# First layer of a four-layer decoder: the end of the gated delta rule moves from a block of its own into the rounds of the loop before it

## The reference, cut to what matters

```
z = (hidden_states @ W_z).reshape(b_, t_, HV, DV)
...
o = oT.transpose(1, 0, 2, 3)
var = jnp.mean(o * o, axis=-1, keepdims=True)
o = o * jax.lax.rsqrt(var + EPS) * norm_w * jax.nn.silu(z)
return o.reshape(b_, t_, V_DIM) @ W_out
```

## Time and profile before

| what | us |
|---|---|
| time, median of 3 runs (lowest to highest) | 4789.43 (4788.31 to 4794.76) |
| profiled execution, its own time | 4789.89 |
| its span, first to last instruction | 4788.2 |
| TensorE, VectorE, ScalarE, GpSimd busy | 4042.8, 2461.2, 1544.0, 820.0 |
| from the end of the loop's last write of `v` to L195's start, first pass | 350.28 to 383.22 |

### The profile page before, as it was taken

The page is one execution under the profiler, slowest core; times in us unless marked ns, Lnnn a source line. Parts: engine busy times, 40 slices in busy tenths (PEclk is TensorE's granted clock), DMA queues, the critical chain, the costliest instruction groups (busy, mean ns, idle before and its releaser), DMA issues. The chain is left out here.

```text
span 4788.2 us, 96589 instructions
## 1 busy us (share of the span) xinstructions
PE 4042.8 (84%) x38364; PEld 2472.2 (52%) x38364; DVE 2461.2 (51%) x6030; ACT 1544.0 (32%) x3476; POOL 820.0 (17%) x1436
## 2 busy tenths in 40 slices
PE   6997787898799778789879987878987998787888
PEld 3883343465388334346548733434654873343465
DVE  5664444454566453445456645335545664533554
ACT  3442222341344222234234422223413542222341
POOL 1430000130143000013014300001201430001120
PEclk7999999999799999999979999999997999999999
DMA  2000000000000000000000010000000001000000
GB/s 79 3 3 16 41 18 17 22 35 25 25 3 3 22 36 18 17 22 35 25 25 3 3 56 1 18 18 22 35 25 25 3 3 56 1 18 18 22 35 27
DMA packets 11005, 105.56 MB, mean 22 GB/s; under 512 B 1148, under 2 KB 5552, under 8 KB 6192
## 3 DMA queue, kind: packets, MB, share of 16 engines
q1 hardware_dynamic: 10544, 99.21, 5.4%
HBM read 98.16 MB, written 1.05 MB: 21 GB/s over the span
## 5 line engine op out<-in xcount | busy, mean ns | idle before, releaser
L88 PE MATMUL psum<-ident_bf 128*128 128x512 bf16 x1880 | 522.1, 416 | 206.6 <-DVE l_attn_peak L770 66.9
L88 PEld LDWEIGHTS psum<-ident_bf 128*128 128x128 bf16 x1880 | 184.6, 106 | 471.4 <-issue 161.8
L2926 DVE TENSOR_TENSOR l_attn_xx<-l_attn_xx,psum 128x256 f32<-128x256 f32 x512 | 205.8, 418 | 205.5 <-PE psum L2633 193.0
L2747 ACT ACTIVATE l_attn_ax<-psum 128x128 f32<-128x128 f32 (+1 forms) x768 | 184.9, 279 | 357.1 <-PE psum L2614 242.7
L399 DVE TENSOR_TENSOR l_ffn_hidden<-l_ffn_silu,psum 128x512 f32<-128x512 f32 (+2 forms) x184 | 126.2, 686 | 323.2 <-ACT l_ffn_silu L340 323.1
L94 PEld LDWEIGHTS psum<-streamed_weights,l_ffn_hidden 128*128 128x128 f32 (+2 forms) x1728 | 225.9, 192 | 115.6 <-issue 98.8
L340 ACT ACTIVATE l_ffn_silu<-psum 128x512 f32<-128x512 f32 (+2 forms) x216 | 128.9, 597 | 473.6 <-PE psum L310 473.3
L2629 PE MATMUL psum<-l_attn_ax,l_attn_xx 64*64 64x64 f32 x5120 | 265.0, 222 | 0.0
L2633 PE MATMUL psum<-l_attn_xx,l_attn_ax 64*64 64x64 f32 x5120 | 258.2, 219 | 0.0
L770 DVE TENSOR_REDUCE l_attn_peak<-psum 128x4 f32<-128x2048 f32 (+3 forms) x128 | 185.7, 1487 | 121.2 <-PE psum L688 120.2
L2824 POOL TENSOR_TENSOR l_attn_part<-l_attn_ab,streamed_weights 128x128 f32<-128x128 f32 x640 | 242.6, 415 | 27.4 <-PE psum L2614 27.4
(11 more groups left out here) (514 smaller groups left out, 8146.2 us busy)
## 6 DMA issues: line engine op xcount, KB each, us to landing
streamed_weights<-pack_l_ffn SPq DMA_DIRECT2D x4, 5412.0 KB, 15.7
streamed_weights<-pack_l_ffn SPq DMA_DIRECT2D x4, 3972.0 KB, 12.6
streamed_weights<-pack_l_attn SPq DMA_DIRECT2D x5, 2848.5 KB, 9.5
streamed_weights<-pack_l_xattn SPq DMA_DIRECT2D x4, 2496.0 KB, 8.6
streamed_weights<-pack_l_ffn SPq DMA_DIRECT2D x4, 2192.0 KB, 8.3
streamed_weights<-pack_l_xattn SPq DMA_DIRECT2D x4, 2048.0 KB, 8.5
streamed_weights<-pack_l_ffn SPq DMA_DIRECT2D x4, 1923.0 KB, 8.0
streamed_weights<-pack_l_attn SPq DMA_DIRECT2D x4, 1107.5 KB, 5.0
```

Source lines behind the costliest of these rows:

```text
L88: pe.matmul(self.bank(bank), self.ident_bf[:, :], self.ident_bf[:, :].unsqueeze(1).to_broadcast([P, NT, P]), start=True, stop=True)
L2747: act.activation(ax[b, p, :, :], m.psum[b, p, 0:P].rearrange("p (i t) -> p i t", i=2), ACT.Copy).then_inc(ax_ready, 1)
L2926: dve.tensor_tensor(both, both, m.psum[:, p, P:384], ALU.subtract).then_inc(x_less, 1)
```

## The change

The second block is gone. Its work is written into the order of rounds 2 to 8, and what is left runs after the loop within the same block. The `warm` matmuls are gone too.

- GpSimd: `squares(n - 2)`, 512 columns, at level 1 of rounds 2 to 7, between the `part` of levels 1 and 2; `squares(6)` and `squares(7)` after the loop's rounds.
- VectorE: `reduce(n - 2)` at level 2 of rounds 2 to 8, behind `prep(n + 1, FIRST)` and ahead of the `output` and the subtraction of level 3. In round 7, `roots` of tiles 0 to 2 (48 columns) follow at level 2, `scale(0)` at level 3, `gated(0)` and `scale(1)` at level 4, `scale(2)` at level 5; in round 8, `gated(1)` at level 2 and `gated(2)` at level 4. Behind the loop: `reduce(7)`, `roots` of tile 3, and `scale` and `gated` of it in two halves.
- TensorE: `gate` (one half tile of `z`) twice at level 1 and once each at levels 3 and 5 of round 7, twice each at levels 2 and 5 of round 8; `turn_y` twice each at levels 1 and 4 of round 8. Behind the loop `turn_y(2)`, `project` of tiles 0 to 2, `turn_y(3)`, `project(3)`. Gates and turned outputs share banks 4 and 5 by turns, in the order of the list `LATE`.
- ScalarE: Silu of the gates in round 7 at levels 2, 3, 4 and 6, and in round 8 behind `corrected`; the copies of the turned outputs in round 8 at levels 1 and 4, between `ks` and `corrected`.
- `z` and the turned outputs use buffers of the loop that are free by then.

```diff
+                def gate(t, half):
+                    n = LATE.index(("z", t, half))
+                    if n >= 2:
+                        pe.wait_ge(late_read, n - 1)
+                    pe.matmul(m.bank(4 + n % 2), m.xnT[:, tok(t)], w["z"][:, 512 * half:512 * half + 512], start=True,
+                              stop=True).then_inc(late_psum, 1)
+
+                def turn_y(t, half):
+                    n = LATE.index(("y", t, half))
+                    pe.wait_ge(y_ready, t + 1 + (half if t == NT - 1 else 0))
+                    pe.wait_ge(late_read, n - 1)
+                    for c in range(4):
+                        ins = pe.transpose(m.psum[:, 4 + n % 2, tok(c)], v[:, t, tok(4 * half + c)], m.ident)
+                    ins.then_inc(late_psum, 1)
+
+                def project(t):
+                    pe.wait_ge(late_read, LATE.index(("y", t, 1)) + 1)
+                    for c in reversed(range(8)):
+                        pe.matmul(m.psum[:, OUT, tok(t)], yT[t][:, c, :], w["out"][:, c, :],
+                                  start=t == 0 and c == 7, stop=c == 0, skip_group_check=True)
...
+                def squares(n):
+                    t, g_ = divmod(n, 2)
+                    o = v[:, t, 8 * W * g_:8 * W * g_ + 8 * W]
+                    pool.wait_ge(o_ready, unit(n, 3) + 1)
+                    if n >= 1:
+                        pool.wait_ge(reduced, n)
+                    pool.tensor_tensor(square[:, :], o, o, ALU.mult).then_inc(square_ready, 1)
...
+                def reduce(n):
+                    dve.wait_ge(square_ready, n + 1)
+                    dve.tensor_reduce(var[:, 8 * n:8 * n + 8], square[:, :].rearrange("p (h v) -> p h v", v=W), AX,
+                                      ALU.add).then_inc(reduced, 1)
...
+                        if n >= 2 and l == 2:
+                            reduce(n - 2)
+                        if n == STEPS - 1 and l == 2:
+                            roots(0, NT - 1)
+                        elif n == STEPS - 1 and l == 3:
+                            scale(0)
+                        elif n == STEPS - 1 and l == 4:
+                            gated(0)
+                            scale(1)
+                        elif n == STEPS - 1 and l == 5:
+                            scale(2)
+                        elif n == STEPS and l == 2:
+                            gated(1)
+                        elif n == STEPS and l == 4:
+                            gated(2)
+                reduce(STEPS - 1)
+                roots(NT - 1, NT)
+                for half in range(2):
+                    scale(NT - 1, slice(8 * half, 8 * half + 8))
+                    gated(NT - 1, slice(8 * half, 8 * half + 8))
```

More of the change, by code:

```diff
@@ L2684, in _ @@
                             past(n, add, SECOND)
+                        if n == STEPS - 1 and l == 1:
+                            gate(0, 0)
+                            gate(0, 1)
+                        elif n == STEPS - 1 and l == 3:
+                            gate(1, 0)
+                        elif n == STEPS - 1 and l == 5:
+                            gate(1, 1)
+                        elif n == STEPS and l == 1:
+                            turn_y(0, 0)
+                            turn_y(0, 1)
+                        elif n == STEPS and l == 2:
+                            gate(2, 0)
+                            gate(2, 1)
+                        elif n == STEPS and l == 4:
+                            turn_y(1, 0)
+                            turn_y(1, 1)
+                        elif n == STEPS and l == 5:
+                            gate(3, 0)
+                            gate(3, 1)
+                turn_y(2, 0)
+                turn_y(2, 1)
+                pe.wait_ge(o_ready, UNITS)
+                for t in range(NT - 1):
+                    project(t)
+                for half in range(2):
+                    turn_y(NT - 1, half)
+                project(NT - 1)
             @block.scalar
@@ L2788, in _ @@
                             ks(n - 1, SECOND)
+                        if n == STEPS - 1 and l == 2:
+                            gate(0, 0)
+                        elif n == STEPS - 1 and l == 3:
+                            gate(0, 1)
+                        elif n == STEPS - 1 and l == 4:
+                            gate(1, 0)
+                        elif n == STEPS - 1 and l == 6:
+                            gate(1, 1)
+                        elif n == STEPS and l == 1:
+                            copy_y(0, 0)
+                            copy_y(0, 1)
+                        elif n == STEPS and l == 2:
+                            gate(2, 0)
+                            gate(2, 1)
+                        elif n == STEPS and l == 4:
+                            copy_y(1, 0)
+                            copy_y(1, 1)
+                        elif n == STEPS and l == 5:
+                            gate(3, 0)
+                            gate(3, 1)
+                for t in (NT - 2, NT - 1):
+                    for half in range(2):
+                        copy_y(t, half)
             @block.gpsimd
@@ L2825, in _ @@
                                                over_block(w["levels"][:, l, :]), ALU.mult).then_inc(part_ready, 1)
+                        if l == 1 and n >= 2:
+                            squares(n - 2)
                         if l == 2 and n + 1 < STEPS:
@@ L2833, in _ @@
                             mask(n + 1, SECOND)
+                squares(STEPS - 2)
+                squares(STEPS - 1)
             @block.vector
@@ L2967, in _ @@
                             add(n - 1, SECOND)
-        mid.close()
[L2970 to L2982, removed]
@@ L3044, in stage_l0_attn @@
+                reduce(STEPS - 1)
+                roots(NT - 1, NT)
+                for half in range(2):
+                    scale(NT - 1, slice(8 * half, 8 * half + 8))
+                    gated(NT - 1, slice(8 * half, 8 * half + 8))
+        mid.close()
     return None
```

112 lines of the change are left out of this document (54 added, 58 removed).

## The result

| what | us |
|---|---|
| changed kernel, median of 4 runs (lowest to highest) | 4738.0 (4730.73 to 4747.60) |
| kernel before on the same chip, 4 runs | 4788.87 (4782.75 to 4794.76) |
| ratio, 95% interval | 0.9899 (0.9877 to 0.9921) |
| profiled execution of the changed kernel, own time and span | 4747.60 and 4745.9 |
| changed stage, first level-1 half of round 0 to the next L195, four passes | 248.74, 248.77, 248.55, 248.80 |

The changed kernel is 50.9 us faster, 4738.0 where 4734 was forecast. Its profiled execution is the slowest of its four. The stage starts at 121.72 there and at 119.04 in before, so its first pass begins 2.68 us later than that of before.

The account below looks back on a forecast made before the run. TensorE bounds the loop; behind it 32.94 us are nearly all one chain. With 2.05 us for the rounds, L195 at 369.4 instead of 383.22 saves 13.8 a pass, 55.3 in four, from 4789.89: 4734.6, as median 4734.1; range 4724 to 4756.

Parts of the forecast that it names:

- Squares on GpSimd, 0: Rounds 2 to 7: squares behind level 1's parts on GpSimd cost 0, or 1 us a round if the cover were gone.
- Nothing is late: Rounds 2 to 7: the squares on GpSimd delay no later work, a cost of 0.
- The cover I named: GpSimd idles 7.3 us behind level 2's parts, which are ready at 285.2 and read by the half at 292.4.
- The sum, 0.27 in each of five rounds: Rounds 2 to 6: VectorE's sum takes 0.62, GpSimd's parts cover 0.35, about 0.27 stays; 1.35 us, bounds 0 and 3.1.
- Contention, +0.14 a round: Rounds 2 to 6: squares push GpSimd's parts under both L2868 on VectorE, 0.14 more each round, 0.7 us in all.
- the 2.05 us that I charged to rounds 2 to 6: Rounds 2 to 6 a pass: 1.35 us for the sums plus 0.7 us for contention.
- Rounds 7 and 8: Added gates, roots and products make `r` of FIRST 4.36 later; last `v` at 354.1 instead of 350.28, at full clock.
- The clock: TensorE's clock stays 1.00 from 340 to 366, where before it falls at about 340.9 in round 8.
- Rival A: TensorE's clock falls in round 8: 7.4 us a pass, 29.4 in four, total 4764; chance 0.30.
- Rival B: VectorE's work isn't hidden up to `r` of round 7: 8.7 us more a pass, 35 in four, total 4769; chance 0.12.
- C: Roots make TensorE wait in round 7, clock falls and stays low until the projection: 13 us slower, 4802; chance 0.06.
- Behind the loop: From last `v` at 354.1: tile 3 ready 361.2, three projections done 362.3, last projection ends 366.05, next stage 367.35.

Follow-up runs that it names:

- Sum at level 1: Changed kernel with the sum of rounds 2 to 7 at level 1 instead of level 2 on VectorE: 4710.2 us, ratio 0.9848 to the kernel before.
- sum twice: Changed kernel with each level 2 sum of rounds 2 to 7 done twice on VectorE: 4741.1 us, ratio 0.9898 to the kernel before.
- squares late: Changed kernel with the squares of rounds 2 to 7 behind the sums of level 2 on GpSimd: 4716.8 us, ratio 0.9852 to the kernel before.
- thin round 8: Changed kernel with round 8's turned outputs, gates, their copies and gated(2) moved behind its work: 4749.0 us, ratio 0.992 to the kernel before.
- products behind: Changed kernel with roots and products of tiles 0 to 2, turned outputs and copies behind the loop: 4781.5 us, ratio 0.9985 to the kernel before.

## Why the prediction was right, point by point

**Squares on GpSimd, 0.** Right in size. But "Nothing is late" left out that the squares wait for the outputs of SECOND (2.67 us) and hold the next parts back by that. The cover I named was there: the parts of level 2 are ready at 292.05, and the half that reads them starts at 295.37.

**The sum, 0.27 in each of five rounds.** Measured 0.27 in round 6 by the idle time ahead of level 4's half. Sum at level 1 gives back 0.25 to 0.26 in rounds 2 and 4 to 6 but 0.58 in round 3, and sum twice shows that no cover is left for a second one in the same four rounds. So the term is right for four of the five rounds; round 3 went its own way in both runs.

**Contention, +0.14 a round: wrong in sign.** The step "the squares push the parts of level 2 under both L2868 of a round" failed. The waiting squares push them beyond both: the first fell from 0.42 to 0.29, and the round gained 0.12 to 0.16. This gain begins at the end of round 1, which is 0.16 shorter. The mechanism itself, a VectorE instruction with two operands in SBUF that runs long while GpSimd works, is borne out by squares late (0.41 again). How long depends on where it begins: at level 3, L2868 began 0.08 us into a single GpSimd part of 0.42 in round 6 and took 0.48; the sum pushes its successor L2986 to 0.31 us into one of 0.41, and it takes 0.28. The roots in round 7 (0.42 and 0.33 beside GpSimd against 0.19) ran long too, with one operand. The Trainium skill (GPSIMD Engine Reference, Specifications) says that GpSimd shares its SBUF interfaces with VectorE and names two cases of contention: VectorE instructions with two SBUF inputs, and those in a 2-port mode. By that rule L2986 agrees (0.41 beside GpSimd, 0.29 alone); the first two instructions of the roots have a single input, so they fall under it only if they ran in such a mode, which no run here shows. Of the 2.05 us that I charged to rounds 2 to 6, the start of round 7 shows 0.44 (197.32 us behind the first half, 196.88 before; 0.23 to 0.62 in the other passes). By the rounds that is five sums at 0.27 less six gains of 0.15.

**Rounds 7 and 8.** From the start of round 7 to the end of the last `v` 38.09 us passed, 38.18 were forecast. `r` of FIRST starts 28.03 us into round 7, where the schedule (343.75 on before's 315.92) had 27.83. The 3.5 us of the roots came out at 3.44. From the stage's start `r` of FIRST is 5.0 us later than before, where 6.4 was forecast.

**The clock.** 1.00 from 340 to 366 as forecast. Rival A was a real mechanism and not a wrong fear: thin round 8 and products behind bring it back. Its price of 7.4 us was not measured by itself. Rival B charged 15.1 us up to `r` of FIRST and is out by the 5.0 measured; products behind puts roots and four products at 0.73 of them. C is out by the clock.

**Behind the loop.** 13.33 us from the end of the last `v` to L195, forecast 13.25. By its parts: tile 3 ready 7.3 us behind the last `v` (7.1), the third projection done 8.2 behind it (8.2), the last projection 2.05 (1.85). The forecast's terms (362.3, 1.0, 0.77, 1.85) add up to 365.92 and not to the 366.05 written, so that 0.13 of the agreement is a slip.

**The sum.** The stage gained 15.4 us a pass, 13.8 were forecast: 1.6 more, which is the 2.05 that became 0.44. L195 stands at 370.46, on before's clock 367.8, where 369.4 was forecast. Over the program the gain is 61.5 instead of 55.3. The median gained 50.9 and the second run of the same kernel 62.9. The 1.7 us a pass that the untouched next stage took more, 7 in all, I had not in the sum at all. So the mechanism was right, but that the total came so near 4734 is in part luck: 6 us too little gain in the stage and 7 us of loss behind it cancel, and the rest is within the scatter between executions, which is as large.

## What to carry to other kernels

When a serial tail is moved into a loop, ask of each moved instruction what it waits for, not only how long it takes: a wait on an idle queue cost nothing here and even took a neighbour's work out of another engine's way. Work placed into the bottleneck engine's short waits can be worth more than its own time, because it keeps the clock: undoing it cost 6 us a pass here, of which at most some 4.6, by the estimate above, are the clock. Before an edit that takes something out is read as its price, look whether the clock stayed the same: in products behind it did not. And read the stages that were not touched: they differed by up to 31 us between kernels, so that an edit of 1 to 2 us a pass has to be judged by its own stretch of the trace, in every pass, and not by the total.

## What the hardware showed that was not expected

- The same unchanged eleven stages took 3274 to 3306 us by kernel, with the same instructions, and 3292 and 3303 in two executions of one kernel. The one behind the change jumps between values from 39.6 to 43.9 as TensorE's clock stands at 1.2 or 2.4 GHz in some stretch, and in all 48 passes this goes with where the stage begins against the moments at which the clock changes.
- One wait of TensorE of 1.21 us did not bring the clock down where two gates followed it; one of 1.01 followed by small products did, within 2 us.
- Two one-operand VectorE instructions on 48 columns took 0.42 and 0.33 us while GpSimd worked; the next one, behind GpSimd's last part, took 0.19.
- A table load of ScalarE took 1.28 us; the Silu behind it started 0.02 us after its end.
